# Wider rows for the turned probabilities, a 128-key tile transposed on TensorE, two tiles normalised on GpSimd, and new orders

## What is computed

```python
xn = layernorm(x)                                   # (4, 512, 256)
Q = xn @ Wq + bq; K = xn @ Wk + bk; V = xn @ Wv + bv # 16, 4, 4 heads of 128
attn = softmax(Q K^T / sqrt(128) + causal mask)
ctx = attn @ V
y = gelu(ctx @ Wo + bo)
s = layernorm(xn + y) * gamma + beta
g = silu((silu(xn @ Wg) * (xn @ Wu)) @ Wd)           # feed-forward, 1024 wide
out = x + s * g
```

## Time and profile before

| what | value |
|---|---|
| median of three runs | 708.92 us |
| the profiled execution, its own time | 708.16 us |
| its span, first to last instruction | 706.4 us |
| PE, DVE, ACT, POOL busy | 89%, 71%, 60%, 36% |
| mean granted TensorE clock | 0.956 |
| DMA: 130,870 packets, 121.35 MB | mean 172 GB/s over the span |
| attention, first scores to the end | from about 163 us to 706.4 us |

### The profile page before, as it was taken

One profiled execution on the slowest core, in us unless ns is written; L12 is line 12 of the kernel. 1 busy time (PEld: TensorE's weight loads), 2 busy tenths in 40 slices (PEclk: granted clock), 3 DMA queues, 4 the chain that ended last, 5 costly groups with the idle time before them and its releaser, 6 DMA issues.

```text
span 706.4 us, 10602 instructions
## 1 busy us (share of the span) xinstructions
PE 625.7 (89%) x3342; PEld 532.6 (75%) x3342; DVE 503.5 (71%) x1119; ACT 421.4 (60%) x1023; POOL 255.9 (36%) x211
## 2 busy tenths in 40 slices
PE   6999999997898897999998889989897999989461
PEld 4788888886786785889787778878776888777351
DVE  4735555437785786889895868988676988978346
ACT  2533444437666665669666477876565687676240
POOL 0000000000335261525476162647544353775244
PEclk9999999999999999899999989999998999999696
DMA  7420121003978889796967989787979888798860
GB/s 254 139 82 30 61 89 59 31 1 113 222 177 204 233 198 227 194 214 170 247 163 208 235 205 242 194 196 190 238 193 237 197 203 232 187 208 225 201 143 30
DMA packets 130870, 121.35 MB, mean 172 GB/s; under 512 B 16256, under 2 KB 112640, under 8 KB 128768
## 3 DMA queue, kind: packets, MB, share of 16 engines
q1 hardware_dynamic: 130128, 120.37, 68.3%
q10 hardware_dynamic: 688, 0.33, 0.2%
HBM read 74.39 MB, written 46.27 MB: 171 GB/s over the span
## 4 chain that ended last, share of the span: by engine, by line
PE 41%; DMA 29%; DVE 10%; SPq 6%; ACT 6%; issue 4%; POOL 2%; DVEq 0%; ACTq 0%; POOLq 0%
PE bank L925 13%; DMA probs<-p_scratch 11%; DMA i_scratch<-inv 9%; DMA p_scratch<-probs 8%; PE down_ps L925 6%; PE down_ps L965 6%; PE bank L954 6%; PE bank L952 6%; SPq L455 5%; DVE probs L864 4%; PE down_ps L1039 4%; ACT probs L651 3%; DMA raw<-in_wgu 2%; POOL pT_lo L532 2%; ACT pT_hi L659 1%
## 5 line engine op out<-in xcount | busy, mean ns | idle before, releaser
L532 POOL TENSOR_TENSOR pT_lo<-probs,pT_hi 128x512 fp32r<-128x512 f32 x160 | 203.4, 1296 | 341.0 <-ACT pT_hi L659 340.4
L659 ACT ACTIVATE pT_hi<-probs 128x512 fp32r<-128x512 f32 x160 | 95.3, 624 | 120.3 <-DMA probs<-p_scratch 99.0
L651 ACT ACTIVATE probs<-probs,least 128x512 f32<-128x512 f32 (+3 forms) x256 | 140.4, 552 | 4.9 <-DVE least L851 4.9
L851 DVE CUSTOM_DVE_ANT_0 probs<-bank,mask 128x512 f32<-128x512 f32 (+3 forms) x256 | 115.7, 485 | 11.8 <-PE bank L925 10.9
L864 DVE STREAM_TRANSPOSE probs<-probs 128x2048 f32<-128x2048 f32 (+1 forms) x64 | 95.7, 1496 | 21.5 <-ACT probs L651 21.5
L925 PE MATMUL down_ps<-pT_lo,v_hi 128*128 128x512 f32 x160 | 69.5, 434 | 45.3 <-POOL pT_lo L532 45.1
L1039 PE MATMUL down_ps<-wo_lo,cT_hi 128*128 128x256 f32 x256 | 74.6, 291 | 10.4 <-DVE cT_lo L883 10.4
L878 DVE TENSOR_TENSOR down_ps<-down_ps,inv_b 128x512 f32<-128x512 f32 x64 | 68.8, 1075 | 16.9 <-DMA inv_b<-i_scratch 8.7
L870 DVE SCALAR_TENSOR_TENSOR qT_lo<-bank,bias,qT_hi 128x512 fp32r<-128x512 f32 x64 | 47.7, 746 | 44.9 <-ACT qT_hi L645 44.5
L925 PEld LDWEIGHTS down_ps<-pT_lo,v_hi 128*128 128x128 f32 x160 | 31.4, 196 | 61.4 <-POOL pT_lo L532 58.3
L1039 PE MATMUL down_ps<-wo_hi,cT_lo 128*128 128x256 f32 x256 | 73.0, 285 | 0.0
(11 more groups left out here) (123 smaller groups left out, 1364.6 us busy)
## 6 DMA issues: line engine op xcount, KB each, us to landing
p_scratch<-probs SPq DMA_DIRECT2D x16, 1024.0 KB, 5.2
probs<-p_scratch SPq DMA_DIRECT2D x64, 256.0 KB, 6.3
inv_b<-i_scratch SPq DMA_DIRECT2D x64, 256.0 KB, 5.0
p_scratch<-probs SPq DMA_DIRECT2D x16, 768.0 KB, 9.6
probs<-p_scratch SPq DMA_DIRECT2D x64, 192.0 KB, 4.3
p_scratch<-probs SPq DMA_DIRECT2D x16, 512.0 KB, 7.9
probs<-p_scratch SPq DMA_DIRECT2D x64, 128.0 KB, 4.9
p_scratch<-probs SPq DMA_DIRECT2D x16, 256.0 KB, 4.4
```

The source lines that it names most:

```text
L532: nc.gpsimd.tensor_tensor(lo[:], turned(t)[:, j], f32(hi[:]), ALU.subtract).then_inc(probsT_split, 1)
L651: nc.scalar.activation(p, p, ACT.Exp, bias=least[:, u, g:g + 1], scale=-1.0, accum_out=total[:, n * T + t, g:g + 1]).then_inc(exp_done, 1)
L659: nc.scalar.activation(pT[(pair_no - 1) % PT_BUFFERS][0][:], turned(t)[:, j], ACT.Copy).then_inc(probsT_hi, 1)
L851: nc.vector.tensor_tensor_reduce(out=blocks_view(t)[:, g], in0=ps[:, 0:(t + 1) * P].rearrange("p (k i) -> p k i", i=BLOCK), in1=mask[:, (T ...
```

## The change

1. **Row width of the turned units.** Units of tiles 1, 2 and 3 (`BY_DRAM`) still go through DRAM. Their columns now stand in quarter order: first the keys whose place within a 128-key tile is 0 to 31 (for all key tiles), then 32 to 63, and so on. The order is made by giving the scores product its keys through a strided view, and by a mask with the same order of columns. A read-back then moves, per partition, four runs of (t+1)×128 numbers, instead of 4(t+1) runs of 128 numbers.
2. **Tile 0** (`T`, `pd`, `no`) doesn't go through DRAM. GpSimd multiplies its probabilities with the reciprocals (`no0`), TensorE transposes them head by head into a ring bank (`T0.0`), ScalarE makes the high part (`ph0.0`) from PSUM, and VectorE the low part (`pd0.0`). Its tt, W, R, IW, IR, c and pl are gone.
3. **Tile 1** is also normalised on GpSimd (`no1`), before its turn on VectorE (tt1 now waits for it). Its IW, IR and c are gone.
4. **New orders** for all five lists.
5. The mask is larger (1280 columns, one part for each tile) and is loaded later, in the feed-forward part.

The diff, cut to its core:

```diff
 TRANSFER_ORDER = """
-W2- IR3- IW1- IW2- W1- R2- W0- IR2- R1- R0- W3 LX@3 IW0- IR1- IW3 ST--@0 IR0- R3
+R1- LX@3 W3 ST-@3 R3 W2 IW2 IW3 W1 R2 IR3 IR2
 """
...
+BY_DRAM = (1, 2, 3)
+NORMED = (0, 1)
...
     def turned_back(i, t, q):
-        return p_scratch[i][t].rearrange("(a i) (j q) n -> q i j a n", a=BLOCKS, q=BLOCKS)[q]
+        return p_scratch[i][t].rearrange("(a m) (q n) -> q m a n", a=BLOCKS, q=BLOCKS)[q]
...
+        def normalised(n, t):
+            pool.wait_ge(inv_made, INVERTED["ri", n, t])
+            at = inv[:, n % KV * T + t, :]
+            if t in BY_DRAM:
+                p = by_blocks(t)
+                factor = at.rearrange("p (k g i) -> p k g i", k=1, i=1).to_broadcast([P, BLOCKS * (t + 1), G, BLOCK])
+            else:
+                p = probs[t][:].rearrange("p (g n) -> p g n", g=G)
+                factor = at.rearrange("p (g n) -> p g n", n=1).to_broadcast([P, G, (t + 1) * P])
+            nc.gpsimd.tensor_tensor(p, p, factor, ALU.mult).then_inc(probs_made, 1)
...
                 elif kind == "tt":
                     t = step[2]
-                    dve.wait_ge(exp_done, max(EXPED["e", n, t, g] for g in range(G)))
+                    if t in NORMED:
+                        dve.wait_ge(probs_made, NORMALISED["no", n, t])
+                    else:
+                        dve.wait_ge(exp_done, max(EXPED["e", n, t, g] for g in range(G)))
...
+                elif kind == "pd":
+                    _, n, t, j = step
+                    hi, lo = pT[(PT_USED["P", n, t, j] - 1) % PT_BUFFERS]
+                    dve.wait_ge(probsT_hi, PT_HIGH["ph", n, t, j])
+                    nc.vector.tensor_tensor(lo[:], ring_ps[RING["T", n, t, j][0]], f32(hi[:]),
+                                            ALU.subtract).then_inc(split_here, 1)
...
             if t:
-                last = product(ps[:, 0:width], [w[:, t * P:(t + 1) * P] for w in qT[g]],
-                               [w[:, 0:width] for w in kT], True, True)
+                keys = [w[:, 0:width] for w in kT]
+                if t in BY_DRAM:
+                    keys = [w.rearrange("p (j q i) -> p q j i", q=BLOCKS, i=BLOCK) for w in keys]
+                last = product(ps[:, 0:width], [w[:, t * P:(t + 1) * P] for w in qT[g]], keys, True, True)
...
+        def transposes(step):
+            _, n, t, j = step
+            pe.wait_ge(probs_made, NORMALISED["no", n, t])
+            ps = ring_bank(step)
+            for g in range(G):
+                at = (g * (t + 1) + j) * P
+                last = nc.tensor.transpose(ps[:, g * P:(g + 1) * P], probs[t][:, at:at + P], ident[:])
+            last.then_inc(turned_here, 1)
```

More of the change, by code:

```diff
@@ L52 @@
 TENSOR_ORDER = """
-P3.2- S3.1 S3.2 S3.3 P3.3- O0-- P2.0- P2.1- S2.0 S2.1 S2.2 S2.3 P2.2- O3- S1.0 S1.1 S1.2 P1.0- S0.0 S0.1 S1.3
-P1.1- O2- S0.2 S0.3 V2@0 Q2+ V3@0 P0.0- V0@0 V1@0 Q0+ K+ O1- Q1+ P3.0 Q3+ P3.1 S3.0+
+O2- K+ V2@0 P0.0- Q0+ V0@0 V1@0 Q1+ Q2+ Q3+ P3.0 V3@0 S3.0+ O1- S3.1+ S3.2+ P3.1 P3.2 S3.3+ P3.3 S0.0+ S0.1+
+T0.0 O0- P2.0 S2.0+ P2.1 P2.2 S2.1+ S2.2+ O3 P1.0 S2.3+ S0.2+ S0.3+ P1.1 S1.0+ S1.1+ S1.2+ S1.3+
 """
 SCALAR_ORDER = """
-ph2.1-- e3.1- e3.2- e3.3- ph2.2-- ch3-- ph1.0-- ph1.1-- gelu-@2 ph0.0-- e2.1- ch2-- e2.3- e2.2- e2.0- e1.1-
-e1.3- e1.2- e0.1- e0.0- e1.0- ch1-- vh2@1 qh2 vh3@1 e0.3- e0.2- vh0@1 ph3.0- ph3.1- ph3.2- vh1@1 qh0 ch0-- kh
-ph3.3- qh1 qh3 ph2.0- e3.0
+e3.0 e3.1 ph2.0- ph2.1- e3.2 e3.3 ph2.2- ch3- e0.0 ph1.0- e0.1 ph1.1- ph0.0- gelu-@1 ch2- e2.1 e2.2 e2.0 e2.3
+e1.0 e1.1 e1.3 e1.2 kh+ e0.3 vh2@0 ch1- e0.2 qh0+ vh0@0 ph3.0 ph3.1 vh1@0 qh1+ ph3.2 qh2+ ph3.3 qh3+ vh3@0 ch0-
 """
 VECTOR_ORDER = """
-ql1 m3.0 ql3 m3.1 m3.2 m3.3 nm-@2 c3- ya1-@1 tt3 cl3- m2.1 m2.0 m2.3 m2.2 ri3 c2- m1.0 m1.1 cl2- m1.2 m0.0 m0.1
-m1.3 tt2 m0.2 c1- m0.3 va2@0 ri1 ri2 tt1 vl2@0 cl1- c0- va3@0 xn@3 ql2+ va0@0 vl3@0 va1@0 vl0@0 ya0-@0 st-@1 ri0
-tt0 vl1@0 ql0+ kl+ cl0-
+m1.1 m1.2 m1.3 tt2 ri3 ri1 xn@3 ri2 va2@0 st-@1 kl+ vl2@0 tt1 cl1- va0@0 ql0+ va1@0 vl0@0 nm-@1 vl1@0 ql1+ ql2+
+ri0 va3@0 ql3+ m3.0+ ya0-@0 m3.1+ vl3@0 cl0- m3.2+ m3.3+ c3 m0.0+ m0.1+ tt3+ ya1-@0 cl3 c2 pd0.0 m2.0+ m2.1+
+m2.2+ m2.3+ m0.2+ m0.3+ cl2 m1.0+
 """
 POOL_ORDER = """
-pl2.0-- pl2.1-- out7--@0 pl2.2-- pl1.0-- out0-@3 pl1.1-- pl0.0-- out1-@3 out2-@3 res-@2 out3-@3 out4-@3 out5-@3
-pl3.0- pl3.1- pl3.2- pl3.3- root-@2 out6-@3
+pl2.1-- pl2.2-- out0-@3 pl1.0-- pl1.1-- out1-@3 out2-@3 res-@2 out3-@3 out4-@3 no1- out5-@3 root-@2 pl3.0-
+pl3.1- pl3.2- pl3.3- out6-@3 out7-@3 no0- pl2.0-
 """
 TRANSFER_ORDER = """
-W2- IR3- IW1- IW2- W1- R2- W0- IR2- R1- R0- W3 LX@3 IW0- IR1- IW3 ST--@0 IR0- R3
+R1- LX@3 W3 ST-@3 R3 W2 IW2 IW3 W1 R2 IR3 IR2
 """
@@ L87 @@
 UNITS = PERIODS * T
+BY_DRAM = (1, 2, 3)
+NORMED = (0, 1)
+MASK_AT = [P * t * (t + 1) // 2 for t in range(T + 1)]
 def words(text):
@@ L123, in ring_of @@
 def ring_of(steps):
-    uses = [s for s in steps if s[0] in ("K", "Q", "S", "V")]
+    uses = [s for s in steps if s[0] in ("K", "Q", "S", "V", "T")]
     return {s: (i % RING_BANKS, uses[i - RING_BANKS] if i >= RING_BANKS else None) for i, s in enumerate(uses)}
@@ L151 @@
 SCALED = ranks(DVE_STEPS, "c")
+INV_USE = SCALED
 CTX_HIGH = ranks(ACT_STEPS, "ch")
@@ L234, in build @@
     v_s = pair("v", [P, T, KV * E])
-    probs = [sb(f"probs{t}", [P, BLOCKS * (t + 1), G, BLOCK]) for t in range(T)]
+    probs = [sb(f"probs{t}", [P, G * (t + 1) * P]) for t in range(T)]
+    mask = sb("mask", [P, MASK_AT[T]])
     pT = [pair(f"pT{i}", [P, G * P]) for i in range(PT_BUFFERS)]
@@ L439, in _ @@
         load_attention(7)
+        sp.wait_ge(part_split, ALL_PARTS)
+        sp.dma_start(mask[:], mask_in).then_inc(mask_in_sem, 16)
         store_g(2)
@@ L975, in ring_bank @@
                 pe.wait_ge(masked, MASKED[("m", *used[1:])])
+            elif used and used[0] == "T":
+                pe.wait_ge(split_here, PT_SPLIT_HERE[("pd", *used[1:])])
             elif used and used[0] == "V":
@@ L1017, in values @@
             unit = UNIT_OF[n, t]
-            pe.wait_ge(probsT_split, PT_SPLIT["pl", n, t, j])
+            if t in BY_DRAM:
+                pe.wait_ge(probsT_split, PT_SPLIT["pl", n, t, j])
+            else:
+                pe.wait_ge(split_here, PT_SPLIT_HERE["pd", n, t, j])
             if n % KV == 0 and t == T - 1:
@@ L1052, in steps @@
                     scores(step)
+                elif step[0] == "T":
+                    transposes(step)
                 elif step[0] == "P":
@@ L1112 @@
     keys = np.arange(P)
-    mask = np.zeros((P, L), np.float32)
-    mask[:, L - P:] = np.where(keys[None, :] > keys[:, None], np.float32(MASK), np.float32(0))
+    masks = []
+    for t in range(T):
+        tile = np.zeros((P, t + 1, BLOCKS, BLOCK), np.float32)
+        tile[:, t] = np.where(keys[None, :] > keys[:, None], np.float32(MASK), np.float32(0)).reshape(P, BLOCKS, BLOCK)
+        masks.append((tile.transpose(0, 2, 1, 3) if t in BY_DRAM else tile).reshape(P, -1))
+    mask = np.concatenate(masks, axis=1)
     arrays = {
```

96 lines of the change are left out of this document (61 added, 35 removed).

## The result

The changed kernel takes 652.09 us (median of four runs, 651.46 to 652.30); the kernel before, beside it, 710.59. The ratio is 0.9172 (95% interval 0.9133 to 0.9211): 8.3% faster, about 59 us. The forecast was 674 us, 5% faster. The direction was right, and so was the place (the periods of attention); the size was not.

The account below looks back on a forecast made before the run. Transfers in a 31.7 us loop were taken to bound attention. 169.4 + 15×29.85 + a tail of 55 gave a span of 672.1 us, with overheads 674; own range 662 to 688, 8 in 10 from 652 to 702.

Parts of the forecast that it names:

- Bound before: Attention in the kernel before: a loop of transfers, 31.6 us, bounds the period, against PE's own 27.8 us on average.
- The three periods without V at 29.0 us: Attention periods lacking V: put at 29.0 us, between PE's 26.9 and the old 31.7, for in-order lists, table loads and clock.
- One in four periods with V: Mean attention period: one V period of 32.4 us to three of 29.0, giving 29.85 us over 15 periods.
- The walk of the loops, 25 us: New lists followed from tile 3's turn: both arms close at about 25 us, below PE's 28.3.
- Engine time of the reads: DMA in attention: 14.1 us per period after, from 23.9, with reads at 401 instead of 178; share near 0.5.
- The worth of the width: Wider read-backs land in 3.5 us instead of 6.6; forecast 674 us, against 687 if width buys nothing.
- PE-bound throughout: Rival for attention: loops close at 25 us and PE alone sets the period; 656 us in its heading; chance 0.10.
- Width buys nothing: Rival on read-backs: reads still land in 6.6 us, a loop of about 30.5 us, 687 us in all; chance 0.12.
- The tile-0 hop: Rival on DVE: pd0, waiting for ph0 on ACT, closes a longer loop of 32.4 us; 718 us; chance 0.11.
- Strided keys: Rival on PE: score passes take twice the time, so PE needs 34.5 us per period; 754 us; chance 0.05.
- GpSimd: Work per period rises from 12.6 to 15.0 us, with no1 at 2.41 us and no0 at 1.26.
- Fill and tail: Before and after the 15 periods: first turn 0.5 us later, at 169.4 us; tail 55 us instead of 61.9.

Follow-up runs that it names:

- e2: Kernel before with only the quarter order of the keys (wide read-backs), old orders, all four tiles through DRAM: 697.0 us, ratio 0.978.
- e5: Kernel before with one change on ACT: tile 3's first two exponentials stand ahead of ph2.0 and ph2.1: 702.5 us, ratio 0.9897.
- e13: Kernel before with SP's list changed in one place, so no reciprocals stand between tile 3's write and read-back: 708.0 us against 715.3, ratio 0.9905.
- e14: Kernel before with wide reads, the exponentials' swap on ACT and the reciprocals' move on SP together, four tiles through DRAM: 690.8 us, ratio 0.9675.
- e4: Changed kernel with one of three passes left out in K, Q, scores and P, output less exact: 628.4 us, ratio 0.8839.
- e16: Changed kernel with the four nm operations moved behind ql1 and ql2 on VectorE: 649.2 us, against 653.3 unchanged on the same chip.
- e10: Changed kernel with one of three passes left out in K, Q, scores and P, and with 512-byte reads: 642.5 us, ratio 0.9071.
- e9: Kernel before with new lists and wide reads, all four tiles through DRAM, tile 0 read back ahead of tile 3's next write: 727.2 us, ratio 1.0248.
- e1: Changed kernel with only the quarter order of the keys undone, so read-backs move 512-byte runs again: 656.8 us, ratio 0.9242.
- e3: Changed kernel with each of the four transposes of a period done twice into the same bank: 657.2 us, ratio 0.9225.

## Why the prediction was wrong in size, step by step

- **Bound before: right.** The chain that ended last runs through the very loop of the earlier trace rows, W3 to W3, by the landing of the first reciprocals, R3's issue, the landing of W2, R2's issue and landing, e3 and tt3:

```profile
454.74 5.67 DMA i_scratch<-inv
...
463.75 9.35 DMA p_scratch<-probs
...
475.07 4.47 DMA probs<-p_scratch
```

Each edit of one of its waits (e2, e5, e13) gave 1% to 2%, and all three together (e14) 3.3%. But e5 and e13 gave a third of what this one loop promised, so others lie close behind it.

- **The three periods without V at 29.0 us: wrong; this is the step that failed.** The allowance of 2.1 us over PE's own 26.9 should have been near nothing. The periods are 27.2, 27.2 and 28.6. Over the 12 such intervals the mean is 27.4, and this makes 19 us of the miss of 22 in span. "Slack of 2 to 3 us is little for five in-order lists" was a guess that no row bore. e4 shows slack of 2 us in the quiet periods, and that was enough: PE's only waits from 195 to 585 us are the three of 1.2 us for ql1. The GELU period is 1.4 us longer, and e16 shows that this came from nm's place and not from the table loads alone. The third ground, that the clock falls after each gap, doesn't hold either: in the kernel before, PE is busy for 27.41 of the 30 us from 225 to 255, and the granted clock there is 1.00.
- **One in four periods with V: wrong by count.** The 15 intervals hold three V periods (those of the first batch row lie ahead of the first turn), not 3.75: 2.6 us too much. The V period itself was right, 32.5 against 32.4.
- **The walk of the loops, 25 us: right in six periods,** 25.2 in e4, and in part by luck, since its parts were off on both sides: W3 lands in 3.9 us (5.2 taken), the reads of R3 are issued in 1.7 (2.6) and land in 4.9 (3.5). For the GELU period and those with and ahead of V it was 2 to 4 us too short.
- **Engine time of the reads: wrong.** The forecast was a DMA share near 0.5, or 14.1 us per period; the windows show 0.57 to 0.86, or about 20 us. I took the rate of 8 KB writes for 2 KB reads, and both rates (401 and 178) from windows of 2 us. The narrow reads cost more than the wide, but by 2.5 us of engine time per period and not 7.4. The Trainium skill ("DMA: Bandwidth & Descriptors", section "Specifications") gives 512 B as enough for line rate. The runs don't agree with it as to the engines' work, 405 us narrow against 365 wide. As to the time it was nearer than I had allowed: in the new lists the width moves it by 0.7%, and by 14 us only where PE covers less (e10 against e4).
- **The worth of the width: too high.** The forecast lay 13 us below the rival in which it buys nothing. It is 16 us alone in the old lists, but 5 us in the new ones. The larger part of the gain came with the new lists and the tiles taken off SP's list together; in e9, lists of that kind with all four tiles on it lose. How this part divides between lists and tiles stays open: my lists didn't work with all four tiles through DRAM, and tile 0's way over TensorE was not run under the old lists.
- **Rivals.** "PE-bound throughout" (656 in its heading, 655 by its sum) was right, and near in its number: 652. I gave it 0.10 because no in-order list in the trace had reached it, which is what the old lists did under another bound. "Width buys nothing" was half right: the width does buy little here, but the 687 rested on a loop of 30.5 us, and e1, with narrow reads, takes 657. The tile-0 hop didn't close: DVE waits for ph0 once, for 0.5 us. Strided keys cost nothing measurable (e1).
- **GpSimd:** no1 and no0 took 1.90 and 1.05 us, less than the 2.4 and 1.26 forecast. **Fill and tail:** 169.3 (169.4 forecast) and 53.9 (55).

## What to carry to other kernels

When a walk of all loops says that the longest closes below the bound engine's own work, forecast that engine's work, and add only for the periods in which a named loop lengthens (here nm in front of ql1). A general allowance for in-order lists was wrong here by 19 us. Price a step that leaves a serial queue by what the queue's list may then look like: the lags between its stages, not the step's own duration. And before an effect of transfers is called the cause, ask how much of it lies under the other engine's work: the same narrow reads cost 5 us with PE's full work and 14 with a quarter less.

## What the runs showed of the hardware

- A TENSOR_SCALAR on VectorE, 128x256 in SBUF, took 400 ns alone and up to 1470 ns beside GpSimd's low parts (rows of L836 above), which took 1.30 us each meanwhile, as elsewhere. Its place decided its price by a factor of three.
- One of the four DMAs of a read-back took 0.43 us to issue on SP with runs of 1 to 2 KB and 0.62 us with runs of 512 bytes (medians of 192 each, in the changed kernel and in e1).
- An fp32 transpose of probabilities on PE took 0.11 us: four more per period made it 0.45 us longer (e3). The moving side in runs of 32 numbers went as fast as contiguous ones: 1.40 against 1.39 us for six score passes (the changed kernel and e1).
